# Two-layer attention kernel on one core: the first layer's turns, its normalization on GpSimd and the order of its queues are rearranged

## The reference

```python
# layer 0, per image row; g = group norm of x over 32 groups of channels
x = _layernorm(g, norm_w, norm_b)
qkv = (x @ qkv_w.T).reshape(*x.shape[:-1], c, 3 * h)          # c = 32, h = 8
aff = jnp.einsum('bmich,bmjch->bmijh', q, k)
gate = jax.nn.sigmoid(x @ gate_w.T + gate_b)
weights = jax.nn.softmax(aff + (x2d @ x2d_w.T * factor)[:, None], axis=-2)
out = jnp.einsum('bmrch,bmirh->bmich', v, weights) * gate
x = x + out.reshape(*x.shape[:-1], c * h) @ final_w.T + final_b
```

## Time and profile before

| | us |
|---|---|
| median of the runs | 3649.43 |
| lowest and highest of 3 runs | 3649.16, 3661.97 |
| the profiled execution | 3664.15 |
| its span from the first to the last instruction | 3662.3 |
| TensorE busy in the span | 3372.3 (92%) |
| VectorE busy | 3002.9 (82%) |
| ScalarE busy | 2776.3 (76%) |
| GpSimd busy | 2177.9 (59%) |

### The profile page before, as it was taken

How to read it: one execution, slowest core, us unless ns; L and a number is a source line. 1 busy time by engine, 2 the same in 40 slices (tenths; PEclk the granted TensorE clock), 3 DMA queues, 4 the chain that set the end, 5 groups by cost and what they waited for, 6 DMA issues and landing times.

```text
span 3662.3 us, 122873 instructions
## 1 busy us (share of the span) xinstructions
PE 3372.3 (92%) x36747; PEld 3007.4 (82%) x36747; DVE 3002.9 (82%) x10850; ACT 2776.3 (76%) x8999; POOL 2177.9 (59%) x4107
## 2 busy tenths in 40 slices
PE   4459999999999999999999999799999999999999
PEld 1148888888888888888888888699999999999998
DVE  4458988888888888888888888688888888888887
ACT  1148888988888888888888988567667677776776
POOL 0047777777777777787777777444444444444443
PEclk7569999999999999999999999899999999999999
DMA  9921111111111111111111111011111111111111
GB/s 341 349 100 54 46 49 51 44 52 45 50 52 43 52 46 48 52 43 52 46 48 50 44 52 44 30 53 52 52 52 52 52 53 54 53 52 52 52 52 47
DMA packets 189032, 238.42 MB, mean 65 GB/s; under 512 B 11824, under 2 KB 176176, under 8 KB 184752
## 3 DMA queue, kind: packets, MB, share of 16 engines
q1 hardware_dynamic: 184368, 204.17, 17.7%
q10 hardware_dynamic: 4608, 33.56, 2.5%
HBM read 170.57 MB, written 67.11 MB: 65 GB/s over the span
## 4 chain that ended last, share of the span: by engine, by line
PE 58%; ACT 14%; issue 11%; DMA 6%; DVE 6%; POOL 2%; DVEq 1%; SPq 1%; ACTq 1%; POOLq 0%
PE work L477 24%; ACT prob L722 7%; PE work L486 7%; PE turn L527 5%; PE score L617 5%; PE mix L650 4%; DMA x_chunk<-xT 4%; PE mix L539 3%; PE score L505 3%; DMA x_tok<-x_nat 3%; PE turn L634 3%; ACT xnT L741 2%; ACT probT L728 2%; PE turn L635 2%; PE turn L636 2%
## 5 line engine op out<-in xcount | busy, mean ns | idle before, releaser
L364 POOL TENSOR_SCALAR prob<-prob,row_inv 128x256 f32<-128x256 f32 x2048 | 1068.0, 540 | 206.1 <-DVE row_inv L932 204.9
L722 ACT ACTIVATE prob<-prob,row_min 128x256 f32<-128x256 f32 x2048 | 1028.1, 507 | 128.3 <-DVE row_min L926 123.6
L477 PE MATMUL work<-src,w 128*128 128x256 f32 x7680 | 1067.5, 288 | 10.4 <-DVE src L915 6.7
L477 PEld LDWEIGHTS work<-src,w 128*128 128x128 f32 x7680 | 951.0, 189 | 12.3 <-DVE src L915 7.4
L415 POOL TENSOR_SCALAR prob<-prob,row_inv 128x160 f32<-128x160 f32 x1024 | 391.0, 401 | 767.4 <-DVE row_inv L1042 767.4
L926 DVE CUSTOM_DVE_ANT_0 prob<-score,neg_bias 128x256 f32<-128x256 f32 x2048 | 749.5, 417 | 17.2 <-PE score L505 10.1
L527 PE MATMUL turn<-ident,prob 128*128 128x128 f32 x3072 | 484.8, 280 | 120.0 <-ACT probT L728 101.4
L789 ACT ACTIVATE prob<-prob,row_min 128x160 f32<-128x160 f32 x1024 | 431.4, 426 | 141.7 <-DVE row_min L1035 141.6
L527 PEld LDWEIGHTS turn<-ident,prob 128*128 128x128 f32 x3072 | 336.3, 141 | 233.2 <-ACT probT L728 125.6
L477 PE MATMUL work<-att,wf 128*128 128x256 f32 x3072 | 432.1, 290 | 4.4 <-DVE att L981 3.0
L486 PE MATMUL work<-w,src 128*128 128x256 f32 x3072 | 425.8, 288 | 0.0
(11 more groups left out here) (110 smaller groups left out, 6225.7 us busy)
## 6 DMA issues: line engine op xcount, KB each, us to landing
pair_chunk<-pairT ACTq DMA_DIRECT2D x32, 1024.0 KB, 8.0
x_chunk<-xT SPq DMA_DIRECT2D x32, 1024.0 KB, 8.5
x_tok<-x_nat SPq DMA_DIRECT2D x128, 256.0 KB, 3.3
x_sb<-xT SPq DMA_DIRECT2D x128, 256.0 KB, 3.4
x1T<-y_sb SPq DMA_DIRECT2D x128, 256.0 KB, 2.2
x_sb<-x1T SPq DMA_DIRECT2D x128, 256.0 KB, 2.9
outT<-y_sb SPq DMA_DIRECT2D x128, 256.0 KB, 2.2
prob<-w_d SPq DMA_DIRECT2D x1, 1024.0 KB, 8.2
```

Source lines behind the costliest of these rows:

```text
L364: pool.tensor_scalar(prob[:, h, ib], prob[:, h, ib], row_inv[:, h, ib:ib + 1], 1.0, ALU.mult, ALU.mult).then_inc(norm_done[0], 1)
L477: ins = pe.matmul(out[:, cb], w[:, of_w, kb, cols + cb * P:cols + (cb + 1) * P], x[:, of_x, kb], start=n == 0, stop=n == len(terms) - 1)
L722: act.activation(prob[:, h, ib], prob[:, h, ib], ACT.Exp, bias=row_min[:, h, ib:ib + 1], scale=-1.0, accum_out=row_sum[:, h, ib:ib + 1]).t ...
```

## The change

All of it is in the first layer.

- TensorE: heads 1, 3 and 6 of a row are turned into the score bank, the others into `turn`; the waits follow from that. Head 1 comes directly after head 0, ahead of `xn`; head 6 directly after head 5, ahead of the projection of `att`.
- ScalarE: the copy of head 6 reads the score bank. The exponentials of head 5 stand ahead of `xnT`, the high half of k ahead of that of `src`, exponentials 6 and 7 and the copy of head 4 ahead of the high half of `att`, the copy of v and the gate; the copy of head 6 follows the gate, and the exponentials of the next row's heads 0 to 2 stand together at the end.
- VectorE: the minima of head 7 follow the copy of head 1; the copy of head 3 stands ahead of k's low half; the low half of `att` comes behind the next row's minima of heads 0 and 1; the layer norm's statistics ahead of the minima of heads 2 and 3. The statistics of y are taken one in each row: the first half of the channels in the row in which the pair of rows is complete, the second half at the start of the row after.
- GpSimd: the power and `xn` move from the start of the body, where they are of row m + 2, to a place ahead of the next row's first pair of heads, where they are of row m + 3.
- SyncE: the load of `x_tok` moves ahead of the wait for `y_sb`.

```diff
 # SyncE, rows()
+                    if n == 0 and ahead.exists:
+                        wait(sp, gn_scaled, ahead.times(1, -1))
+                        sp.dma_start(x_tok[:, ahead.base % 2], ...)
                     if last.exists:
                         wait(sp, y_done[n], m.times(1 if n == 0 else CB))
...
 # GpSimd: norms(m, 1), product, norms(m, 2), sum, norms(m, 3), then
+                if ahead.exists:
+                    wait(pool, ln_var_done, ahead.times(2, 2))
+                    pool.tensor_tensor(ln_rstd[:], ln_var[:], minus_half[:], ALU.pow)
...
+                        pool.tensor_scalar(xn[:, tb], g_tok[:, ahead.base % 2, tb], ln_rstd[:, tb:tb + 1], ...)
                 if nxt.exists:
                     norms(nxt, 0)
 # TensorE, scores()
-                    wait(pe, turn_done[0][1], r.times(PAIRS0, 2 * hg - 2))
+                    if hg == 0:
+                        wait(pe, turn_done[0][1], r.times(PAIRS0, -2))
+                    else:
+                        wait(pe, turn_done[0][0], r.times(PAIRS0, 0))
 # TensorE, turns()
-                    if h % HPG == HPG - 1:
+                    if h in (1, 3, 6):
                         to = score[:, 0].rearrange("p b t -> p (b t)")
+                    if h == 0:
+                        wait(pe, turn_done[0][1], m.times(PAIRS0, 0))
+                    elif h == 1:
+                        wait(pe, min_done[0], m.times(TB * H0, TB * (HPG + 1)))
+                    elif h == 2:
+                        wait(pe, turn_done[0][0], m.times(PAIRS0, 1))
+                    elif h == 3:
+                        wait(pe, turn_done[0][1], m.times(PAIRS0, 1))
+                    elif h == 4:
+                        wait(pe, turn_done[0][0], m.times(PAIRS0, 2))
+                    elif h == 5:
+                        wait(pe, turn_done[0][0], m.times(PAIRS0, 3))
+                    elif h == 6:
+                        wait(pe, turn_done[0][1], m.times(PAIRS0, 2))
+                        if nxt.exists:
+                            wait(pe, min_done[0], nxt.times(TB * H0, TB))
...
 # ScalarE, body0()
-                    turn_copy(0)
+                    turn_copy(0, turn[:])
+                    exps(m, 5)
                 if far.exists:
...
+                if m.exists:
+                    turn_copy(6, score[:, 0].rearrange("p b t -> p (b t)"))
+                if nxt.exists:
+                    exps(nxt, 0)
                     exps(nxt, 1)
 # VectorE, body0()
+                def out_stats(ob, r, pair):
+                    wait(dve, y_done[0], r.times(1, 1))
+                    dve.bn_stats(gstat1[:, ob, at], y_sb[:, ob]...).then_inc(y_stats, 1)
                 if done.exists:
+                    if done.base % 2 == 0 and (done + -1).exists:
+                        out_stats(1, done + -1, done.times(1, -1, of=2))
...
                     inverse(m, 2)
+                if done.exists and done.base % 2 == 1:
+                    out_stats(0, done, done.times(1, 0, of=2))
+                if m.exists:
+                    turn_copy(3, score[:, 0].rearrange("p b t -> p (b t)"))
                 if nxt.exists:
                     wait(dve, k_high[0], nxt.times(1, 1))
...
+                if nxt.exists:
+                    mins(nxt, 2)
+                    mins(nxt, 3)
+                    inverse(nxt, 0)
+                if m.exists:
+                    turn_copy(7, turn[:])
```

More of the change, by code:

```diff
@@ L316, in body @@
                     last, far, ahead = m + -1, m + 3, m + 4
+                    if n == 0 and ahead.exists:
+                        wait(sp, gn_scaled, ahead.times(1, -1))
+                        apart(sp, sp_passed)
+                        sp.dma_start(x_tok[:, ahead.base % 2], x_tok_v[:, bass.ds(ahead.times(TB), TB), :]
+                                     ).then_inc(x_tok_in[ahead.base % 2], 16)
                     if last.exists:
@@ L554, in body0 @@
                     turns(0)
+                    turns(1)
                 if far.exists:
@@ L743, in body0 @@
                                        ).then_inc(xnT_done, 1)
+                if nxt.exists:
+                    wait(act, k_ps[0], nxt.times(1, 1))
+                    act.copy(kT[:, nxt.base % 2, HIGH], work[:, 0]).then_inc(k_high[0], 1)
+                if far.exists:
                     wait(act, xnT_done, far.times(CB, CB))
@@ L747, in body0 @@
                 if m.exists:
[L748 to L753 removed]
+                    turn_copy(2, turn[:])
+                    exps(m, 6)
+                    exps(m, 7)
+                    turn_copy(4, turn[:])
                 if last.exists:
@@ L988, in body0 @@
                     mins(nxt, 1)
-                    mins(nxt, 2)
-                if m.exists:
-                    turn_copy(5, turn[:])
-                if nxt.exists:
-                    mins(nxt, 3)
-                if nxt.exists:
-                    inverse(nxt, 0)
+                if last.exists:
+                    wait(dve, att_high[0], last.times(1, 1))
+                    dve.tensor_tensor(att[:, LOW], att_sum[:], att[:, HIGH].bitcast(F32), ALU.subtract
+                                      ).then_inc(att_done[0], 1)
                 if ahead.exists:
@@ L1011, in body0 @@
                     dve.tensor_scalar(ln_var[:], ln_mv[:, :, 1], EPS, None, ALU.add).then_inc(ln_var_done, 1)
-                if done.exists and done.base % 2 == 1:
-                    wait(dve, y_done[0], done.times(1, 1))
-                    apart(dve, dve_passed)
-                    for ob in range(CB):
-                        pair = done.base // 2
-                        at = slice(pair, pair + 1) if done.loop is None else bass.ds(done.times(1, 0, of=2), 1)
-                        dve.bn_stats(gstat1[:, ob, at], y_sb[:, ob].rearrange("p r t -> p (r t)")).then_inc(y_stats, 1)
+                if nxt.exists:
+                    mins(nxt, 2)
[3 more added lines that the diff above has]
+                    turn_copy(7, turn[:])
             over_rows(dve, 3, 2, body0)
+            dve.wait_ge(y_done[0], ROWS)
+            dve.bn_stats(gstat1[:, 1, ROWS // 2 - 1:ROWS // 2], y_sb[:, 1].rearrange("p r t -> p (r t)")).then_inc(y_stats, 1)
             dve.wait_ge(y_stats, CB * ROWS // 2)
```

75 lines of the change are left out of this document (21 added, 54 removed).

## The result

| | us |
|---|---|
| the changed kernel, median of 4 runs (lowest, highest) | 3565.20 (3560.69, 3568.42) |
| the kernel before, median of 4 runs beside them | 3653.14 |
| ratio, 95% interval | 0.9755 (0.9732 to 0.9778) |
| forecast, range | 3562, 3512 to 3650 |
| the profiled execution, its span | 3564.76, 3562.9 |

The change makes the kernel 2.4% faster, by 88 us. In the two traces the sums of the second group norm, TensorE's last steps of the first layer, start at 2352.61 before and at 2252.95 after, 99.7 earlier, and the spans differ by 99.4, so nothing is won behind the first layer. Of the 99.7, 8.05 lie ahead of it, where the change does nothing: the same sums of the first group norm start at 211.94 and 203.89. The first layer itself is 91.6 shorter.

What follows compares the result with a forecast made beforehand. No engine is full; queues wait for each other in a ring. A row was to fall from 16.35 to 15.16 + 0.5 = 15.66 us, 87 us less over 126 rows, giving 3562 us, range 3512 to 3650.

Steps and rivals of the forecast that it cites:

- The floor of 15.16: TensorE's time for one first-layer row without waits, in us: a short row's 15.63 less 0.47 of waiting at head 1.
- the waits at head 1: TensorE's transposes of head 1 wait for ScalarE's copy of head 0: 0.47 in short rows, 1.28 more every second row.
- the long wait: At head 1 every second row, 1.28 us: two statistics of y on VectorE delay head 4's minima, then ScalarE's copy.
- cover: In the score bank, head 1 wants VectorE's minima of head 4 only 1.2 us after they are done.
- the ScalarE rival: Head 5's exponentials ahead of xnT make the v projection wait 0.65 every second row: 3603 us, chance 0.16.
- its 1.5 us: GpSimd's wait per row for the load of x_tok, 169.6 us in 114 cases, claimed to go.
- The 0.5 that was left: Waits a row left of 1.19: 0.1 for k's chain, 0.3 for head 6, 0.1 for att's low half.
- the prediction's own list of a row: TensorE's expected start times within a row without waits, counted from the q projection to the end at 15.16 us.
- the chain through k: Head 3's copy, then k's low half, on VectorE before the next scores: ready at 9.7 against 9.67, charged 0.1 a row.
- Att's low half, put at 0.1: On VectorE, ending at 13.1 to 13.4 us for a y projection due at 13.3, charged 0.1 a row.
- the two low halves against the factors: VectorE's low halves of src and att hold GpSimd's factors, some 0.5 to 0.7 each; head 6 late, charged 0.3.
- The rival with GpSimd's sum: GpSimd's sum blocks VectorE's src low half for 1.30, so VectorE needs 16.31 a row: 3644 us, no change, chance 0.13.

## Why the prediction was right, and where it was not

**The frame held.** The floor of 15.16 was never undercut, the waits at head 1 went, and 15.65 a row came out where 15.66 was forecast. The median is 3 us from the forecast. One sign that was to show it did not come: the rows were to lie within 0.3 of each other, and they lie 0.43 apart where head 6 waits.

**Statistics:** right. The prediction had the long wait go because head 1 has cover, and it went. Undoing the split alone gave 28 us, against 30 in the expectation of that run, and the wait at head 1 in every second row is where it came.

**The bank:** its direct cost was right (0.6 a row on undoing it). That it brings anything needs the other parts, which the prediction did not say; ScalarE's order stands in it only as a risk (xnT late, the ScalarE rival). The runs on the kernel before showed the other side: with the old order the stall only moves to the scores, and with ScalarE's order of these three the short rows win what the long ones lose. The rival itself didn't happen: no wait for xnT is among the waits of the changed kernel.

**x_tok:** right in kind, and without a price. The prediction let its 1.5 us go "from GpSimd, not from TensorE", because TensorE hardly waited for GpSimd in the old order. It added that the time "pays for what follows", but set no price on that: in the new order it is 127 us, more than the whole gain. What the early load brings alone on the kernel before was not run.

**The 0.5 that was left:** right as a sum (15.65 - 15.16 = 0.49), and part of that is luck, since its terms are off both ways. I compare distances from start to start, as means of the trace, with the prediction's own list of a row. The scores come 0.24 later behind v, where the chain through k was put at 0.1: the handover to TensorE takes 0.34 where 0.05 was assumed, and the run with the waits turned round showed that the place of k's wait makes most of that. Head 6 comes 0.25 later behind head 5, near the 0.3 of the prediction: in about a third of the rows it waits 0.43 (0.14 a row on the list of waits), and some 0.1 in the others stays below what that list shows. Another 0.1 lies in y and head 7 behind it, and places elsewhere that run some 0.1 faster than the prediction's list make up for it. Att's low half, put at 0.1, doesn't appear among TensorE's waits. The cause of head 6's wait was only half seen: less the two low halves against the factors than the inverse behind the low half.

**The rival with GpSimd's sum:** its mechanism came true in every second row and its price did not. I called its sign a median near 2 us; it is 1.59, and that is the median of two kinds of rows, some 1.6 and some 0.8 to 0.9. By the rule of the Trainium skill, "SBUF — State Buffer", section "SBUF: two separate sides", that the later of the two blocks fully, the low half ends only after the sum: in the rows above the sum ends at 1229.69 and the low half at 1230.23, so the trace agrees. But the rival added 1.30 to VectorE's work in every row, where the low half loses 0.56 on average. The same stretch holds VectorE's wait for the scores, which it had itself put at 0.4 and which measures up to 0.9; two waits in one place overlap, and the longer one counts. That it is harmless here is luck of the place: in the run of the split alone the same collision, on att's low half, came with the loss of the gain.

## What to carry to other kernels

When queues of about equal load wait for each other in a ring, the share of one wait says little about what its removal brings: taken alone on the kernel before, two of the parts brought nothing, and undone one by one four parts cost 308 us, where the whole brings 88. Price an edit by what stands next in each queue, in the new order, and look for time on an idle engine as the thing that pays. And order the waits ahead of an instruction so that the one that is late stands last; here that alone moved the time by less than the intervals tell apart, until the next late place was mended too.

## What the runs showed of the hardware that was not expected

- The place of a wait among several has a price. With k's wait ahead of two others the scores started 0.34 behind its release; with it last, 0.14 (in the run of that alone the low half runs from 1216.17 for 0.68, the scores start at 1216.99, where v's product ends too).
- A VectorE instruction with two operands in SBUF (src's low half, 0.68 alone) takes up to 1.73 beside GpSimd's sum in the changed kernel. It goes the other way too: the sum, 1.29 at its usual, took 1.71 beside the two low halves in the run of the split alone.
